# A perceiver block with eight experts: output rows gathered, added to and scattered back after each expert, and slots transposed by VectorE

## The reference

```
logits = xf @ gate_w.T; probs = softmax(logits)
top_p, top_i = top_k(probs, 2);  w = top_p / sum(top_p)
rank  = cumsum(one_hot(top_i)) - 1          # per choice k, over the tokens
keep  = rank < 160                          # capacity of one expert, per choice
for e in range(8):
    y   = (silu(xf @ gate_proj_w[e].T) * (xf @ up_proj_w[e].T)) @ down_proj_w[e].T
    out = out + comb[:, e] * y              # comb = w * keep where the token chose e
```

## Time and profile before

| | |
|---|---|
| median of 3 runs | 1029.68 us (1029.11 to 1032.28) |
| the profiled execution | 1030.8 us, of which the span from first to last instruction is 1029.1 us |
| granted TensorE clock, mean | 0.997 of full speed |
| PE busy | 1010.3 us, 98% |
| DVE, ACT, POOL busy | 609.0 us, 392.3 us, 195.3 us |
| expert stage, first L896 to last L912 | 657.2 to 1014.3 us |
| end, behind the last L912 | 1014.3 to 1029.1 us |

### The profile page before, as it was taken

One profiled execution on the slowest core, in us unless ns is written; L12 is line 12 of the kernel. 1 busy time (PEld: TensorE's weight loads), 2 busy tenths in 40 slices (PEclk: granted clock), 3 DMA queues, 4 the chain that ended last, 5 costly groups with the idle time before them and its releaser, 6 DMA issues.

```text
span 1029.1 us, 14116 instructions
## 1 busy us (share of the span) xinstructions
PE 1010.3 (98%) x5263; PEld 767.6 (75%) x5263; DVE 609.0 (59%) x1174; ACT 392.3 (38%) x626; POOL 195.3 (19%) x180
## 2 busy tenths in 40 slices
PE   7999899999999999999999999999999999999998
PEld 4884444444454568878888888899999999999997
DVE  6358433435656566896475675676565565655666
ACT  2222112212111143355757632544444444445441
POOL 2003300002000036455322125700000000000051
PEclk9999999999999999999999998999999999999999
DMA  8709489999999922023210101865454545535443
GB/s 296 301 1 397 193 344 410 408 411 390 411 401 402 374 79 71 4 91 115 93 46 31 31 8 57 309 242 179 154 184 146 204 152 175 197 129 178 148 144 133
DMA packets 38567, 206.90 MB, mean 201 GB/s; under 512 B 5312, under 2 KB 6848, under 8 KB 34288
## 3 DMA queue, kind: packets, MB, share of 16 engines
q1 hardware_dynamic: 33312, 187.95, 49.1%
q0 software_dynamic: 5200, 18.22, 5.1%
HBM read 190.04 MB, written 16.12 MB: 200 GB/s over the span
## 4 chain that ended last, share of the span: by engine, by line
PE 94%; DVE 4%; ACT 1%; issue 1%; DMA 0%; SPq 0%; DVEq 0%; ACTq 0%
PE ps L470 28%; PE ps L896 22%; PE ps L912 11%; PE ps L627 9%; PE ps L598 8%; PE ps L464 3%; PE ps L490 2%; PE ps L580 1%; PE ps L608 1%; PE ps L631 1%; PE ps L937 1%; PE ps L789 1%; PE ps L882 1%; PE ps L516 1%; PE ps L640 1%
## 5 line engine op out<-in xcount | busy, mean ns | idle before, releaser
L896 PE MATMUL ps<-x,w 128*128 128x320 f32 x1536 | 237.2, 310 | 1.1 <-DVE x L1849 1.1
L896 PEld LDWEIGHTS ps<-x,w 128*128 128x128 f32 x1536 | 228.5, 188 | 5.1 <-issue 1.4
L1799 DVE TENSOR_TENSOR w<-big,w 128x1536 fp32r<-128x1536 f32 x64 | 112.5, 1759 | 91.6 <-ACT w L1199 91.0
L912 PE MATMUL ps<-w,hsplit 128*128 128x512 f32 x512 | 128.9, 394 | 0.0
L1199 ACT CAST w<-big 128x1536 fp32r<-128x1536 f32 x64 | 94.4, 1478 | 40.1 <-PE ps L912 40.1
L912 PEld LDWEIGHTS ps<-w,hsplit 128*128 128x128 f32 x512 | 93.2, 188 | 16.6
L598 PE MATMUL ps<-big 128*64 128x512 f32 (+2 forms) x512 | 98.1, 499 | 1.7 <-DVE ps L1420 1.1
L470 PE MATMUL ps<-xcT,u 128*128 128x512 f32 x432 | 98.2, 389 | 0.0
L470 PEld LDWEIGHTS ps<-xcT,u 128*128 128x128 f32 x432 | 81.0, 188 | 17.0 <-DVE xcT L1587 0.2
L627 PE MATMUL ps<-big 128*64 128x512 f32 x384 | 89.5, 599 | 2.1 <-DVE big L1434 0.5
L598 PEld LDWEIGHTS ps<-big 128*64 128x64 f32 x512 | 45.6, 136 | 49.6 <-issue 42.0
(11 more groups left out here) (330 smaller groups left out, 1495.1 us busy)
## 6 DMA issues: line engine op xcount, KB each, us to landing
big<-in_ctxT SPq DMA_DIRECT2D x16, 3202.0 KB, 16.8
big<-in_ctx SPq DMA_DIRECT2D x16, 3072.0 KB
big<-in_w_units SPq DMA_DIRECT2D x64, 768.0 KB, 4.3
big<-in_dense_units SPq DMA_DIRECT2D x41, 256.0 KB, 2.7
xs<-big POOLq DMA_DIRECT2D x1, 5120.0 KB, 17.3
big<-in_gate_units SPq DMA_DIRECT2D x12, 384.0 KB, 3.0
hr<-xs SPq DMA_DIRECT2D x7, 512.0 KB, 5.0
ys<-big POOLq DMA_DIRECT2D x7, 512.0 KB, 3.3
```

The lines of the kernel that those rows point to most:

```text
L896: mm = nc.tensor.matmul(ps[:, 2 * part + f % 2, 0:SLOTS], wsplit[f % RING][w][:, c:c + P], xsplit[j][x][:, d, :], start=(d == 0 and w + x ...
L912: mm = nc.tensor.matmul(ps[:, 4 + s, :], x, w, start=(f == 0 and k == 0), stop=(f == FC - 1 and k == len(terms) - 1))
L1799: V.tensor_tensor(wsplit[f % RING][1][:], wraw[f % RING], wsplit[f % RING][0][:].bitcast(F32), ALU.subtract).then_inc(w_low, 1)
```

## The change

**Results.** `ys`, its gathers, `pick_last`, the transposes of picks and `last_rows` are gone. The output tensor itself is now the accumulator: as soon as the second layer is done SP stores the token rows `xr` to `out` (8 DMAs, and 2 more to 320 spare rows behind the 1024, so that each is defined). Each slot learns its token row and its weight: DVE writes pairs (row + 1, weight) into `token_meta`, POOL scatters them by 16 indirect DMAs of 8 bytes a row into a DRAM table `tab`, with the same index as `xs`, waits, loads the table back by slot (`slot_meta`, 3 DMAs of 8-byte pieces), and DVE turns it into `row_from` and `row_to` (empty slots write to spare rows). Then, for each expert: POOL gathers the 320 output rows (3 indirect DMAs), DVE adds the weighted results (`mix`), POOL scatters them back (3 indirect DMAs) and waits for the landing before the next expert's gathers. Expert 0's results are held in SBUF and mixed in step 2 of expert 1, since the table is not there yet. In the last expert `down(7)` does the groups in the order 0, 2, 1.

**Slots.** DVE transposes 32 by 32 blocks (`turn_slots`, one instruction for each group) instead of PE's 128 by 128. The blocks stay in the partitions that they came from, so the rows are loaded in another layout (4 DMAs of 512-byte pieces instead of 2 of 2 KB) and the gate and up weights of experts 1 to 7 are stored with permuted rows. ACT and DVE now read the turned slots from SBUF.

DVE's code for experts 3 to 6 is written out instead of looped.

```diff
@@ sync
             def load_rows(n, j):
                 rows = xs[bass.ds(n * SLOTS, SLOTS), :]
-                load(xe[j][:, 0:NS - 1, :], rows[0:(NS - 1) * P, :].rearrange("(s p) d -> p s d", p=P), xe_in[j])
-                load(xe[j][0:LAST, NS - 1, :], rows[(NS - 1) * P:SLOTS, :], xe_in[j])
+                for q in range(P // Q):
+                    load(xe[j][q * Q:(q + 1) * Q, :, :], rows[:, q * P:(q + 1) * P].rearrange("(s r) w -> r s w", r=Q), xe_in[j])
...
             load_rows(1, 1)
+            out_rows = out[0:T, :].rearrange("(i p) d -> p i d", p=P)
+            for i in range(NT):
+                wait_evacuated(sp, "wo", i)
+                sp.dma_start(out_rows[:, i, :], xr[:, i, :]).then_inc(out_begun, 16)
+            sp.dma_start(out[T:T + 2 * P, :].rearrange("(i p) d -> p i d", p=P), xr[:, 0:2, :]).then_inc(out_begun, 16)
+            sp.dma_start(out[T + 2 * P:T + SLOTS, :], xr[0:LAST, 2, :]).then_inc(out_begun, 16)
@@ tensor
-                    if last:
-                        transpose_picks(f)
                     down(n, f, first, last and f == FC - 1)
-                    turns = (3, 4, 5) if first else (1, 3, 4)
-                    if f in turns and not last:
-                        transpose_slots(nxt, 1 - j, turns.index(f))
@@ vector
+            def mix(n, s, y, signal):
+                m = slots_of(s)
+                return V.scalar_tensor_tensor(mixed_rows[0:m, s, :], y, slot_meta[0:m, n, s, 1:2], mixed_rows[0:m, s, :],
+                                              ALU.mult, ALU.add).then_inc(signal, 1)
+            def mix_held():
+                dve.wait_ge(mix_in, 16 * NS)
+                for s in range(NS):
+                    mix(0, s, held[0:slots_of(s), s, :], held_mixed)
+            def mix_results(n, order=range(NS), last=False):
+                dve.wait_ge(mix_in, 16 * NS * (n + 1))
+                if not last:
+                    dve.wait_ge(down_done, n * FC + FC)
+                for k, s in enumerate(order):
+                    if last:
+                        dve.wait_ge(last_done, k + 1)
+                    if s == NS - 1:
+                        dve.wait_ge(tail_high, n + 1)
+                        mix(n, s, ytail[0:LAST, :], mix_step)
+                        dve.wait_ge(mix_step, n)
+                    mix(n, s, ps[0:slots_of(s), 4 + s, :], y_evac)
...
+            def turn_slots(n, j, s, loads):
+                if s == 0:
+                    dve.wait_ge(xe_in[j], loads * 64 + 64)
+                b = slice(s * 4, min(s * 4 + 4, SB))
+                V.transpose(turned[j].rearrange("p c (s r) -> p s c r", r=Q)[:, b, :, :],
+                            xe[j][:, b, :].rearrange("p s (c r) -> p s c r", r=Q)).then_inc(xt_done, 1)
...
-                    if f == 0 and not first:
-                        results_out(n - 1, 1 - j, half)
+                    if f == 0 and n == 1:
+                        hold_results()
+                        slot_rows()
+                    if f == 0 and n > 1:
+                        mix_results(n - 1)
+                    if f == 2 and n == 1:
+                        mix_held()
@@ gpsimd
+            for i in range(NT):
+                for k in range(TOPK):
+                    G.indirect_dma_start(tab, bass.IndirectOffsetOnAxis(scat[:, TOPK * i + k:TOPK * i + k + 1], 0),
+                                         token_meta[:, i, k, :], None).then_inc(tab_out, 16)
+            pool.wait_ge(tab_out, 16 * NT * TOPK)
+            slot_tab = tab[0:TRASH, :].rearrange("(n r) w -> r n w", r=SLOTS)
+            for s in range(NS):
+                lo, hi = s * P, min(s * P + P, SLOTS)
+                pool.dma_start(slot_meta[0:hi - lo, :, s, :], slot_tab[lo:hi, :, :]).then_inc(meta_in, 16)
+            pool.wait_ge(out_begun, 16 * (NT + 2))
+            pool.wait_ge(rows_set, 2)
+            for n in range(NE):
+                if n:
+                    pool.wait_ge(mix_out, 16 * NS * n)
+                for s in range(NS):
+                    m = slots_of(s)
+                    G.indirect_dma_start(mixed_rows[0:m, s, :], None, out,
+                                         bass.IndirectOffsetOnAxis(row_from[0:m, n * NS + s:n * NS + s + 1], 0)).then_inc(mix_in, 16)
+                for k, s in enumerate(LAST_ORDER if n == NE - 1 else range(NS)):
+                    m = slots_of(s)
+                    pool.wait_ge(y_evac if n else held_mixed, n * NS + k + 1)
+                    G.indirect_dma_start(out, bass.IndirectOffsetOnAxis(row_to[0:m, n * NS + s:n * NS + s + 1], 0),
+                                         mixed_rows[0:m, s, :], None).then_inc(mix_out, 16)
+            pool.wait_ge(mix_out, 16 * NS * NE)
```

More of the change, by code:

```diff
@@ L450, in _ @@
             expert_loads(NE - 1, 1, last=True)
[L451 to L455, removed]
         @block.tensor
@@ L865, in _ @@
                 first_expert_rows(d, 1)
[L868 to L883, removed]
             def gate_up(n, j, f, first=False):
@@ L904, in down @@
                 h, wh, wl = hsplit[f % 2], wsplit[f % RING][0][:, 2 * DC * P:UW], wsplit[f % RING][1][:, 2 * DC * P:UW]
-                for s in range(NS):
+                for s in LAST_ORDER if final else range(NS):
                     if f == 0 and not first:
@@ L1260, in _ @@
             expert(NE - 1, 1, last=True)
-            picks_out(NT - 1)
-            act.wait_ge(y_out[1], 32 * (NE // 2 - 1))
-            for s in range(NS):
-                act.wait_ge(last_done, s + 1)
-                nc.scalar.copy(y_last[0][:, s, :], ps[:, 4 + s, :]).then_inc(last_high, 1)
+            tail_out(NE - 1, last=True)
         @block.vector
@@ L1835, in expert @@
                         route_weights()
-                    if first and 2 <= f < 2 + NT // 2:
-                        pick_last_rows(2 * (f - 2))
-                    if first and f == FC - 2:
-                        pick_last_again()
-                    turns = (4, 5, 6) if first else (2, 4, 5)
+                    turns = (3, 4, 5) if first else (1, 3, 4)
+                    if f - 1 in turns and not last:
+                        slots_low(n + 1, 1 - j, turns.index(f - 1))
                     if f in turns and not last:
-                        slots_low(n + 1, 1 - j, turns.index(f))
-                    if last:
-                        for i in range(*((0, 0), (0, 0), (0, 0), (0, 1), (1, 2), (2, 4), (4, 7), (7, 8))[f]):
-                            mix(i)
+                        turn_slots(n + 1, 1 - j, turns.index(f), loads)
             def first_expert_low(d):
@@ L1856, in _ @@
             split_low(0, 2)
-            expert(0, 0, first=True)
-            expert(1, 1)
-            expert(2, 0)
-            with dve.Fori(0, NE // 2 - 2) as i:
-                expert(i * 2 + 3, 1, i + 1)
-                expert(i * 2 + 4, 0, i + 1)
-            expert(NE - 1, 1, NE // 2 - 1, last=True)
-            for s in range(NS):
-                dve.wait_ge(last_high, s + 1)
-                V.tensor_tensor(y_last[1][:, s, :], ps[:, 4 + s, :], y_last[0][:, s, :].bitcast(F32),
-                                ALU.subtract).then_inc(last_low, 1)
-            for i in range(NT):
-                dve.wait_ge(last_filled, i + 1)
-                dve.wait_ge(mixed, i + 1)
-                V.scalar_tensor_tensor(xr[:, i, :], ps[:, (0, 1, 2, 3, 7, 0, 1, 2)[i], :], mx[:, i:i + 1], xr[:, i, :],
-                                       ALU.mult, ALU.add).then_inc(out_ready, 1)
+            expert(0, 0, 0, first=True)
+            for n in range(1, NE):
+                expert(n, n % 2, n // 2, last=n == NE - 1)
+            mix_results(NE - 1, LAST_ORDER, last=True)
         @block.gpsimd
```

168 lines of the change are left out of this document (60 added, 108 removed).

## The result

The changed kernel takes 1024.91 us (median of 19 runs, 1019.19 to 1029.78); the kernel before took 1030.76 us beside it (1028.74 to 1034.14, 19 runs). The ratio is 0.9944, 95% interval 0.9930 to 0.9958: 5.8 us faster where 22 were forecast, and outside the range. The profiled execution took 1027.4 us, with a span of 1025.6 us against a forecast of 1006.5.

A forecast was written before the change was run, and what follows sets the result against it. PE's instruction list was taken to bound the expert stage, with the end behind it. The shorter span, -22.6, plus 0.5 for the table gave -22.1 us, hence a forecast of 1008.0 us, range 1004 to 1018.

The forecast's parts named there:

- PE loses 14.2 us: Expert stage: transpositions of seven experts, 11.5 us, and eight steps' picks, 2.8 us, leave PE, all on the path.
- the stage: PE from expert 0's first `gate_up` matmul to expert 7's last: 352.4 us before, forecast 338.9.
- The turn at 0.7 us, DVE hidden: Slot transposition on DVE: 0.7 us per turn of 512 values a partition; DVE's added work never reaches PE.
- Hidden, with 2 us to spare: Ten stores before expert 1's weights: 6 us of SP's issue, weights issued about 681, wanted by ACT about 688.
- the same 3.4 us of slack takes it: Fallback for late weights in expert 1: `hid` may come 3.4 us late before PE's `down` needs its low part.
- The table: DVE's wait in step 0 of expert 1: scattered table back at 708 to 709.5, cost 0 to 1.3 us, taken 0.5.
- The pace of the scatters: POOL's 16 scatters to the table before expert 1's mixing: 1.54 us each, 24.6 us in all.
- The mix in step 2: Expert 1, step 2: 1.7 us of wait for gathers and 2.2 of mixing make `hid(3)` 2.5 us late, hidden.
- The last scatter at D + 6.0, landing 2.5 us: Kernel's end: POOL's last scatter to `out` issued 6.0 us after the last `down` starts, landing 2.5 us later.
- D: Start of the last `down` in expert 7, forecast at 998.04.
- The span's end: End of the kernel: D + 8.5, 1006.5 instead of 1029.1, 22.6 us less, bounds 21 to 24.
- The rival of a longer end: Kernel's end: scatter landing of 4.8 us and mixes waiting for last gathers give D + 11, 1010 to 1011; chance 0.03.

The follow-up runs named there:

- tab_two: The changed kernel with 2 of its 16 scatters to the small table, leaving out the entries of tiles 0 to 6: 1019.78 us, ratio 0.9842 to before.
- best64: The changed kernel with stores moved early, 64-byte table entries, expert 0's mixing one step later and the last wait by SP: 1014.84 us, ratio 0.9837 to before.
- slots_only: The kernel before with only the slots' half of the change (512-byte row pieces, DVE's 32 by 32 transposition, weights to match): 1024.06 us, ratio 0.9897.
- tab64: The changed kernel with 64 bytes in place of 8 per entry of the small table: 1018.37 us, ratio 0.9833 to before.
- early: The changed kernel with its stores to the output issued earlier, the last two around the first expert's weights: 1022.00 us, ratio 0.9906 to before.
- rows_long: The changed kernel with slot rows read as one run of 4608 contiguous bytes per partition, not nine 512-byte pieces: 1024.85 us, ratio 0.9909 to before.
- tab512: The changed kernel with 512 bytes in place of 8 per entry of the small table: 1021.56 us, ratio 0.9865 to before.
- spend: The changed kernel with the last wait, for the last three scatters' landing, made by SP instead of POOL: ratio 0.9916 to before.

## Why the prediction was wrong, point by point

- **PE loses 14.2 us: right.** PE's plain step is 753.29 - 747.94 = 5.35 us, without a transposition anywhere. Where nothing is late (tab_two, best64) the stage is 338.9 us, as forecast; best64's last `down` starts at 997.5, forecast 998.04, on a stage that began 0.6 us earlier than before's. The half done alone (slots_only) gave its share but for the 1.5 us of one wait.
- **The turn at 0.7 us, DVE hidden: right.** 0.704 us, and no pause of PE from 720 to 1000 us.
- **"Hidden, with 2 us to spare", the ten stores ahead of expert 1's weights: the step that failed.** The issue came when I had it (682.48 for 681), but from there to ACT's need at 688 the step left some 7 us for the landing with the 2 to spare in them, so 5 for loads that took 15.3 at the median. The step summed SP's issue alone. Between 680 and 710 us the rest of the stores (2.6 MB in all), the row loads, six weight loads and the table's scatters shared 16 engines. And the packets of the weights took 411 ns on average, not 289, with the 8-byte scatters beside them (tab64: 290). No single one was enough: with the stores moved (early), the row loads in long pieces (rows_long) or the entries at 64 bytes (tab64), each alone, PE had no stall for weights. "If not, the same 3.4 us of slack takes it" failed with it, since PE was late by 6.5 us. Cost in the changed kernel: 348.1 - 338.9 = 9.2 us, the fall of the clock behind the stall in it.
- **The table.** I priced its small entries for their own landing, by the queue's time per piece. Their own packets were cheap (the 64-byte packets in which the trace has them took 19 to 34 ns on average in the changed kernel from 680 to 710 us). What they did to everybody else was not in the sum. The pace of the scatters was as forecast, 1.49 us (675.16 to 697.57, 15 steps) for 1.54; their landing was not, 8.7 us after the last issue for 4. So the table's loads were issued at 707.68, forecast about 700.6 and after; that was hidden only because the stall held DVE up as well, and it was DVE's wait as soon as the stores were moved (early: 3.2 us). The Trainium skill, DMA: Bandwidth & Descriptors, section Specifications, has the DMA engine do read-modify-write below 512 B. No run here shows read-modify-write itself. The harm beside 8-byte entries would fit the rule; 64-byte entries, also below 512 B, cost the weights nothing here (290 ns), and the measurement decides.
- **The mix in step 2, "hidden by 0.9 us":** true in the changed kernel (DVE waited 2.1 us there, PE not at all), but only because the stall had let the gathers catch up. In early, rows_long, tab64 and tab512 PE paid 3.3 to 4.9 us.
- **The last scatter at D + 6.0, landing 2.5 us: right** (D + 6.1 and about 2.8). **The span's end: the second step that failed, by 6.8 us.** The sum let the span end with the last landing; POOL's closing, 7.0 us, begins there and was put at nothing. The rival of a longer end had D + 11 by other causes; it is D + 15.3. The record was in the trace of before, 8.8 us, but in none of the views that I read.
- **Start of the stage, 3.0 us:** the fall of the clock in that profile, and not the change's.

Sum for the profiled execution: 3.0 + (350.05 - 340.84) + (15.3 - 8.5) = 19.0 of the 19.1 us, the stage taken here up to D.

## What to carry to other kernels

Price a small scatter by what the big transfers beside it take, not by its own packets, and look at the mean of those packets, since the median hides it; if entries can be padded to 64 bytes, try that first. When a load is moved behind others, add up the bytes and packets of all queues until it must have landed, not the issue times. And before the last transfer is given to GpSimd, read the closing records behind the last instruction: here 82 ns for each DMA it had ever issued, free as long as another engine ends later.

## What the hardware showed that was not expected

- With 16 scatters of 128 entries of 8 bytes, 6144-byte packets of another queue took 363 to 487 ns on average (289 before); with entries of 64 or 512 bytes 290 and 284 ns. It is a tail: the medians are 234 to 266 ns in all of them, but in the kernels with 8-byte entries single packets took up to 2.1 to 5.0 us, in tab64 and tab512 at most 1.3.
- GpSimd's closing DRAIN: 4.00, 5.87, 7.02 and 8.32 us after 48, 71, 85 and 101 DMAs, where it had waited for the last of them to land.
- The granted clock fell to half, for 3.4 to 10.2 us, at every stall of PE of 3.3 us or more in expert 1 and at some shorter ones (2.0 us in rows_long, 1.8 in spend), while others of 0.5 to 1.5 us had no fall; in the changed kernel the 24 matmuls of a `gate_up` that it caught took 5.94 us instead of 3.68. In some executions it also fell near 640 us, ahead of the expert stage, in kernels made from before and from the changed one alike; what decides that stays open.
